# Second attention of a two-layer decoder: a running minimum, a scale moved into two other instructions, and GpSimd's work in another order

## The chip, the core and the metric
The kernel runs on one core of one Trainium2 chip. The metric is device time in microseconds, the median of three runs. TensorE multiplies matrices into PSUM, VectorE and ScalarE work on whole tiles (128 rows by so many columns) in PSUM or SBUF, GpSimd (POOL in the profile) on SBUF alone, SyncE (SP) issues DMA. Each engine works through its own queue in order and waits on semaphores for the others.

## The reference, cut to what matters
Two pre-norm decoder layers on 2048 tokens of width 256; each is attention and a feed-forward part. The change lies in the attention of the second layer, which has 16 heads over a latent of 64 columns, with a rotary part:

```
kv_c = x @ d_kv_w.T;  q_lat = x @ d_q_w.T          # 64 columns each
q = [u_q(q_lat), rope(qr(q_lat))];  k = [u_k(kv_c), rope(qr(kv_c))]
probs = softmax(q @ k.T / sqrt(128 + 64))           # 2048 x 2048, 16 heads, no mask
out = (probs @ u_v(kv_c)) @ out_w.T
```

## The kernel before, in words
The stage is `second_attention`. `prepare` makes the latents and folds the content part of query and key into one 64x64 matrix per head (`fold_hi`, `fold_lo`). Numbers that need more than one pass of precision are kept as a high part and a rest (`_hi`, `_lo`), so a product of two of them is three matmuls.

The main loop runs over 256 tiles: 16 heads by 16 blocks of 128 query rows. A tile's 2048 scores per row are worked on as two halves of 1024 columns, in a ring of three half-tiles in PSUM (`psS`). For tile n:

- TensorE: `scores(n+1, 0)`, `scores(n+1, 1)` (12 matmuls), one `project` piece of the next head in tiles 0 to 11 of a head, `context(n-2)` (32 pairs' worth of matmuls over the turned probabilities), and in the odd heads `output(n-9)`. Piece kinds 0 and 1 are rotated by VectorE; kind 2 is the fold, three matmuls over the 64 rows of the latent (lines 1585 to 1587).
- VectorE: `half(n+1, 0)` is the minimum of half 0 (the scores are negated) into `lows`; `low(n, 0)` subtracts the high part of half 0's probabilities; `half(n+1, 1)`; `whole_min(n+1)` takes the smaller of the two and adds 14 ln 2 as `shift`, so that the exponentials come out times 2^14; `rotate` for piece kinds 0 and 1; `invert(n-2)`; `low(n, 1)`.
- ScalarE: `exponential(n, 0)` (needs `shift`), `normalise(n-3)`, `take_output(n-10)`, `high(n, 0)` (the high part as f16), `exponential(n, 1)`, roundings and folds of the next head, `high(n, 1)`. `normalise(m)` waits until the splits of all tiles up to m-2 are done, since it writes one of two buffers of `both_sums`.
- GpSimd, the loop at the end of `gpsimd`: it waits for `low(n-1, 1)`, then adds a bias (first head) and an output (`add`), places weights in tile 14, waits for `low(n, 0)`, then one of `add_up` (two sums, `whole` of the queries and `whole_k` of the keys), `rest_queries` or `rest_keys`, by the remainder (i-2) mod 3 of the tile's number i in its head, for i from 2 to 13, and last `split(n-3)`: three small steps on `both_sums` and `ctxp`.
- SyncE: two transposes of the probabilities by DMA per tile, each waits for its `low`.

The subtractions of VectorE (`low`) read two tensors in SBUF; `half` and `rotate` read PSUM.

Of the kernel before, what the change touches and what calls it, by code (L numbers as in the profile page):

```python
# [44 lines left out]
def decoder_two_layers(nc, x_in, wq0, bq0, wk0, bk0, wv, bv, wout, bout, rwT, ewT, eb3, c_pick,  # L45
# [1080 lines left out]
    def second_attention():  # L1126
# [3 lines left out]
        LIFT = 14.0  # L1130
# [9 lines left out]
        fold_hi = sb(L, "fold_hi", [C, 1 + NH, C], F32R)  # L1140
        fold_lo = sb(L, "fold_lo", [C, 1 + NH, C], F32R)
# [28 lines left out]
        def prepare():  # L1170
# [84 lines left out]
            def vector():  # L1255
# [13 lines left out]
                for w in (fold_hi, fold_lo):  # L1269
                    ins = dve.tensor_scalar(w[:, 0, :], ident[0:C, 0:C], 0.0, None, ALU.mult)  # L1270
# [10 lines left out]
                def fold_rest(g):  # L1281
                    heads = slice(1 + 8 * g, 9 + 8 * g)
                    dve.wait_ge(fold_high, g + 1)
                    dve.scalar_tensor_tensor(out=fold_lo[:, heads, :], in0=six[4 + g][0:C, :].rearrange("p (h c) -> p h c", c=C),
                                             scalar=-SCALE, in1=fold_hi[:, heads, :].bitcast(F32), op0=ALU.mult,
                                             op1=ALU.subtract).then_inc(fold_low, 1)
# [61 lines left out]
            def scalar():  # L1348
# [29 lines left out]
                for g in range(2):  # L1378
                    act.wait_ge(fold_ready, g + 1)
                    act.activation(fold_hi[:, 1 + 8 * g:9 + 8 * g, :], six[4 + g][0:C, :].rearrange("p (h c) -> p h c", c=C),  # L1380
# [17 lines left out]
            def gpsimd():  # L1398
# [4 lines left out]
                pool.wait_ge(cleared, 1)  # L1403
                for j in range(NB):
# [47 lines left out]
        lows = sb(L, "lows", [P, 2, 2])  # L1452
# [112 lines left out]
        def tensor():  # L1565
            def project(head, piece):
# [166 lines left out]
        def vector():  # L1733
# [17 lines left out]
            def half(n, g):  # L1751
# [539 lines left out]
```

## Time and profile before
| | |
|---|---|
| time, median of 3 runs | 2437.64 us (2432.28 to 2438.07) |
| the profiled execution: time / span | 2436.7 / 2435.3 us |
| mean granted TensorE clock | 0.981 |
| second attention's main loop | from about 797 to 2240 us |
| busy, share of span | PE 90%, DVE 87%, ACT 75%, POOL 45% |

The rows below are copied from the trace of that execution. A line Lnnn is a line of the kernel before. Row durations of VectorE overlap a little: the next instruction can start before the row of the one before ends.

### The profile page before, as it was taken

To read this page: it belongs to the slowest core of one execution; us is meant where nothing else is said; L and a number is where in the kernel's file an instruction comes from. 1 tells how busy PE (TensorE), PEld (TensorE's weight loads), DVE (VectorE), ACT (ScalarE), POOL (GpSimd) and SP (SyncE) were. 2 spreads that over 40 slices of the span, in tenths; PEclk is the share of its full clock that TensorE was granted. 3 is DMA by queue.
4 is the path that set the end of the run, shared out by engine and by line. 5 is a ranking of instruction groups with operands and counts; after the bars stand their busy time and mean duration, and the time that the engine had idled before them with its cause. 6 is when DMAs were issued, how large, how long until landed. Compare 5 with 4: busy or idle time off the path is not lost.

```text
span 2435.3 us, 50686 instructions
## 1 busy us (share of the span) xinstructions
PE 2201.4 (90%) x18544; PEld 1583.4 (65%) x18544; DVE 2109.6 (87%) x3124; ACT 1822.2 (75%) x2613; POOL 1098.4 (45%) x1464
## 2 busy tenths in 40 slices
PE   4888888889997899999999999999999999988899
PEld 2444444455655667777777777767777777766687
DVE  6888888879987999999999999999999999987421
ACT  4777777745555788889888888888888888877411
POOL 3312111101224577657657667657666656622200
PEclk9999999989998999999999999999999999999899
DMA  3000000041000799999999999999999999999000
GB/s 130 1 2 2 1 1 2 2 87 32 1 1 1 137 193 196 195 193 198 195 195 194 194 195 193 187 194 195 194 198 191 196 196 199 205 195 191 21 18 18
DMA packets 1119318, 300.69 MB, mean 123 GB/s; under 512 B 1107232, under 2 KB 1116416, under 8 KB 1118208
## 3 DMA queue, kind: packets, MB, share of 16 engines
q1 hardware_dynamic: 1116224, 295.21, 69.8%
q8 instruction: 150, 2.46, 0.4%
q10 hardware_dynamic: 2848, 2.23, 0.3%
q14 instruction: 96, 0.79, 0.1%
HBM read 18.45 MB, written 2.10 MB: 8 GB/s over the span
## 4 chain that ended last, share of the span: by engine, by line
PE 28%; DVE 21%; issue 7%; DMA 6%; ACT 5%; POOL 1%; SPq 0%; DVEq 0%; ACTq 0%; POOLq 0%
DVE lows L1757 10%; DVE parts L1773 9%; DMA partsT<-parts 6%; PE psOb L1629 4%; PE psS L1612 4%; PE psS L1709 4%; PE psS L1614 3%; PE psS L1613 3%; ACT prob L1952 2%; PE psOb L1630 2%; PE psOb L1665 2%; ACT parts L1962 2%; PE psOb L1729 1%; PE psPb L1729 1%; PE psPb L1585 1%
## 5 line engine op out<-in xcount | busy, mean ns | idle before, releaser
L1773 DVE TENSOR_TENSOR parts<-prob,parts 128x1024 f16<-128x1024 f32 x512 | 679.9, 1328 | 18.9 <-ACT parts L1962 17.4
L1952 ACT ACTIVATE prob<-psS,shift 128x1024 f32<-128x1024 f32 x512 | 574.8, 1123 | 143.7 <-DVE shift L1765 139.0
L1757 DVE TENSOR_REDUCE lows<-psS 128x1 f32<-128x1024 f32 x512 | 622.4, 1216 | 5.6 <-PE psS L1614 5.0
L1962 ACT CAST parts<-prob 128x1024 f16<-128x1024 f32 x512 | 537.4, 1050 | 30.1 <-DMA partsT<-parts 26.2
L1612 PE MATMUL psS<-k_hi,q_lo 128*128 128x512 f32 x1024 | 446.7, 436 | 82.6 <-ACT prob L1952 75.2
L1629 PEld LDWEIGHTS psOb<-kv,partsT 128*128 128x128 f16 x4096 | 357.0, 97 | 99.0 <-issue 75.7
L1629 PE MATMUL psOb<-kv,partsT 128*128 128x130 f16 x4096 | 398.0, 221 | 20.1 <-DMA partsT<-parts 20.1
L1614 PE MATMUL psS<-k_hi,q_hi 128*128 128x512 f32 x1024 | 407.6, 398 | 0.0
L1613 PE MATMUL psS<-k_lo,q_hi 128*128 128x512 f32 x1024 | 405.5, 396 | 0.0
L1630 PE MATMUL psOb<-kv,partsT 128*128 128x66 f16 x4096 | 387.7, 193 | 0.0
L1630 PEld LDWEIGHTS psOb<-kv,partsT 128*128 128x128 f16 x4096 | 360.5, 98 | 1.0 <-issue 1.0
L665 ACT ACTIVATE PT<-psS 128x1024 bf16<-128x1024 f32 (+1 forms) x320 | 278.6, 899 | 64.8 <-PE psS L409 41.2
L1612 PEld LDWEIGHTS psS<-k_hi,q_lo 128*128 128x128 f32 x1024 | 194.0, 189 | 190.3 <-ACT prob L1952 154.9
L2086 POOL TENSOR_TENSOR both_sums<-both_sums 128x64 f32<-128x64 f32 x256 | 178.5, 697 | 164.3 <-DVE parts L1773 135.8
L1614 PEld LDWEIGHTS psS<-k_hi,q_hi 128*128 128x128 f32 x1024 | 193.7, 189 | 46.0
L1613 PEld LDWEIGHTS psS<-k_lo,q_hi 128*128 128x128 f32 x1024 | 195.2, 191 | 25.4
L737 POOL TENSOR_TENSOR qB<-nmT,blocks 32x512 bf16<-32x512 bf16 x64 | 73.5, 1148 | 301.3 <-DVE qB L540 298.7
L409 PE MATMUL psS<-qB,kT 128*128 128x512 bf16 (+3 forms) x640 | 180.0, 352 | 11.2 <-ACT PT L665 11.0
L524 DVE TENSOR_REDUCE pm<-psT 128x1 f32<-128x512 f32 (+3 forms) x256 | 156.7, 612 | 36.4 <-PE psT L383 23.9
L524 DVE TENSOR_REDUCE pm<-psU 128x1 f32<-128x512 f32 (+2 forms) x255 | 150.1, 589 | 22.8 <-PE psU L383 11.5
L2090 POOL TENSOR_TENSOR ctxp<-both_sums,ctxp 128x64 f16<-128x64 f32 x256 | 140.0, 547 | 20.5
L2056 POOL TENSOR_TENSOR whole<-rot 64x512 f32<-64x512 f32 x64 | 82.7, 1293 | 130.8 <-DVE parts L1773 124.4
(294 smaller groups left out, 3969.6 us busy)
## 6 DMA issues: line engine op xcount, KB each, us to landing
partsT<-parts SPq DMA_TRANSPOSE x512, 4.9
ef<-in_ewT SPq DMA_DIRECT2D x1, 2048.0 KB, 9.7
rf<-in_rwT SPq DMA_DIRECT2D x1, 2048.0 KB, 10.2
outw_s<-in_outwT SPq DMA_DIRECT2D x1, 2048.0 KB, 8.5
trig<-in_trig SPq DMA_DIRECT2D x2, 1024.0 KB, 11.5
out_x<-ot SPq DMA_DIRECT2D x16, 128.0 KB, 1.7
wug<-in_wupT SPq DMA_DIRECT2D x4, 256.0 KB, 3.7
wug<-in_wgateT SPq DMA_DIRECT2D x4, 256.0 KB, 3.9
```

The lines of the kernel that those rows point to most:

```text
L409: ins = pe.matmul(bank, kT[:, pair % 2, m * P:(m + 1) * P], qB[:, h, c * BANK + r * P:(c + 1) * BANK], start=True, stop=not diag)
L524: dve.tensor_reduce(pm[:, h, r, j:j + 1], max_banks[max_place[n["max"]]][:, 0:w], AX_X, ALU.max).then_inc(max_taken, 1)
L665: act.activation(PT[:, h, first:first + width], psS[:, x * BANK:x * BANK + width], ACT.Exp).then_inc(exp_done, 1)
L1612: pe.matmul(bank, q_lo[:, slot, q], k_hi[b][:, k], start=True, stop=False)
L1613: pe.matmul(bank, q_hi[:, slot, q], k_lo[b][:, k], start=False, stop=False)
L1614: ins = pe.matmul(bank, q_hi[:, slot, q], k_hi[b][:, k], start=False, stop=True)
L1629: pe.matmul(psO[:, 0:KW], partsT[:, s, 0, m, :], kv16[:, block, :], start=(block == 0), stop=False)
L1630: ins = pe.matmul(psO[:, 0:REST], partsT[:, s, 1, m, :], kv16[:, block, 0:REST], start=False, stop=(block == NT - 1))
L1757: dve.tensor_reduce(lows[:, n % 2, g:g + 1], psS[:, (2 * n + g) % 3, :], AX_X, ALU.min).then_inc(half_min, 1)
L1773: dve.tensor_tensor(parts[:, s, 1, :], prob[:, g, :], parts[:, s, 0, :], ALU.subtract).then_inc(low_done, 1)
L1952: act.activation(prob[:, g, :], psS[:, (2 * n + g) % 3, :], ACT.Exp, bias=shift[:, n % 2:n % 2 + 1], scale=-1.0).then_inc(exp_done, 1)
L1962: act.copy(parts[:, s, 0, :], prob[:, g, :]).then_inc(high_done, 1)
```

## The change
Four things. (1) `LIFT` is now the factor 2^14, applied as the scale of the cast (`high`, now an activation with Copy) and as the multiplier of the subtraction (`low`, now a multiply-subtract); the exponential itself is not lifted any more. (2) The small instruction `whole_min` is gone: half 0's minimum goes to `lows`, and half 1 is one pass that adds 0 to the scores, writes them back where they stand in PSUM and takes the running minimum from `lows` into its accumulator output, `shift`. (3) The folds run over 128 rows; the lower 64 rows of `fold_hi` and `fold_lo` are cleared by two copies on GpSimd in `prepare`. (4) GpSimd's order: the split of tile n-4 comes behind the second subtraction of tile n-1; the keys' sum is made one tile after the queries', as `add_up_keys`; the additions of outputs stand in one of two places.

```diff
-        LIFT = 14.0
+        LIFT = 2.0 ** 14
-        fold_hi = sb(L, "fold_hi", [C, 1 + NH, C], F32R)
+        fold_hi = sb(L, "fold_hi", [P, 1 + NH, C], F32R)
...
+                for w in (fold_hi, fold_lo):
+                    pool.tensor_copy(w[latent, :, :].rearrange("p a n -> p (a n)"), kvs[rotary, 0:(1 + NH) * C]).then_inc(pool_step.sem, 1)
+                    pool.wait_ge(pool_step.sem, pool_step.next())
...
-                    pe.matmul(bank, fl2, lat_hi[0:C, cols], start=True, stop=False)
-                    pe.matmul(bank, fh2, lat_lo[0:C, cols], start=False, stop=False)
-                    pe.matmul(bank, fh2, lat_hi[0:C, cols], start=False, stop=True).then_inc(piece_ready, 1)
+                    pe.matmul(bank, fl2, lat_hi[:, cols], start=True, stop=False)
+                    pe.matmul(bank, fh2, lat_lo[:, cols], start=False, stop=False)
+                    pe.matmul(bank, fh2, lat_hi[:, cols], start=False, stop=True).then_inc(piece_ready, 1)
...
-                if g == 0 and n >= 2:
-                    dve.wait_ge(shift_ready, n - 1)
-                dve.tensor_reduce(lows[:, n % 2, g:g + 1], psS[:, (2 * n + g) % 3, :], AX_X, ALU.min).then_inc(half_min, 1)
-
-            def whole_min(n):
-                if n >= TILES:
-                    return
-                dve.wait_ge(half_min, 2 * n + 2)
-                if n >= 2:
-                    dve.wait_ge(exp_done, 2 * n - 2)
-                dve.tensor_scalar(shift[:, n % 2:n % 2 + 1], lows[:, n % 2, 0:1], lows[:, n % 2, 1:2],
-                                  LIFT * float(np.log(2.0)), ALU.min, ALU.add).then_inc(shift_ready, 1)
+                here = psS[:, (2 * n + g) % 3, :]
+                if g == 0:
+                    if n >= 2:
+                        dve.wait_ge(shift_ready, n - 1)
+                    dve.tensor_reduce(lows[:, n % 2:n % 2 + 1], here, AX_X, ALU.min).then_inc(half_min, 1)
+                else:
+                    dve.wait_ge(half_min, n + 1)
+                    if n >= 2:
+                        dve.wait_ge(exp_done, 2 * n - 2)
+                    dve.tensor_scalar(here, here, 0.0, lows[:, n % 2:n % 2 + 1], ALU.add, ALU.min,
+                                      accum_out=shift[:, n % 2:n % 2 + 1]).then_inc(shift_ready, 1)
...
-                dve.tensor_tensor(parts[:, s, 1, :], prob[:, g, :], parts[:, s, 0, :], ALU.subtract).then_inc(low_done, 1)
+                dve.scalar_tensor_tensor(out=parts[:, s, 1, :], in0=prob[:, g, :], scalar=LIFT, in1=parts[:, s, 0, :],
+                                         op0=ALU.mult, op1=ALU.subtract).then_inc(low_done, 1)
...
-                act.copy(parts[:, s, 0, :], prob[:, g, :]).then_inc(high_done, 1)
+                act.activation(parts[:, s, 0, :], prob[:, g, :], ACT.Copy, scale=LIFT).then_inc(high_done, 1)
...
+            def add_up_keys(head, j):
                 if (head, j) == (1, 0):
                     pool.wait_ge(keys_rested, NB)
-                for side, (out_rows, rows) in enumerate(((whole, rotary), (whole_k, latent))[:2 if head else 1]):
-                    pool.tensor_tensor(out_rows[rotary, :], rot[0][rows, :], rot[1][rows, :], ALU.add).then_inc(added_up, 1)
-                    pool.wait_ge(added_up, sums(head, j) + side + 1)
+                pool.tensor_tensor(whole_k[rotary, :], rot[0][latent, :], rot[1][latent, :], ALU.add).then_inc(added_up, 1)
+                pool.wait_ge(added_up, sums(head, j) + 2)
...
-            for n in range(TILES + 3):
+            for n in range(TILES):
                 head, i = n // NT + 1, n % NT
                 j, turn = divmod(i - 2, 3)
-                ahead = n < TILES and head < NH
-                if n < TILES:
-                    pool.wait_ge(low_done, 2 * n)
+                ahead = head < NH and 2 <= i <= 13
+                pool.wait_ge(low_done, 2 * n)
+                if ahead and turn == 1:
+                    add_up_keys(head, j)
+                else:
+                    split(n - 4)
                 if n < NT:
                     add_bias(n)
-                add(n - LATER - 1)
-                if ahead and i == 14 and head + 1 < NH:
+                if not (ahead and turn):
+                    add(n - LATER - 1)
+                if i == 14 and head + 1 < NH:
                     take_weights(head + 1)
-                if n < TILES:
-                    pool.wait_ge(low_done, 2 * n + 1)
-                if ahead and 2 <= i <= 13 and turn == 0:
+                pool.wait_ge(low_done, 2 * n + 1)
+                if ahead and turn == 0:
                     add_up(head, j)
-                if ahead and 2 <= i <= 13 and turn == 1:
+                if ahead and turn == 1:
                     rest_queries(head, j, 2 * (n + 1))
-                if ahead and 2 <= i <= 13 and turn == 2:
+                    split(n - 4)
+                if ahead and turn == 2:
                     rest_keys(head, j)
+                if ahead and turn:
+                    add(n - LATER - 1)
+            split(TILES - 4)
+            for n in range(TILES, TILES + 3):
+                add(n - LATER - 1)
                 split(n - 3)
```

## Rows read from the trace of the kernel before

**Rows 1.** Page, part 1: engine, busy us (share of span), instructions
```profile
PE 2201.4 (90%) x18544; PEld 1583.4 (65%) x18544; DVE 2109.6 (87%) x3124; ACT 1822.2 (75%) x2613; POOL 1098.4 (45%) x1464
```

**Rows 2.** Page, part 5: groups; busy us, mean ns of one, idle before, releaser
```profile
L1773 DVE TENSOR_TENSOR parts<-prob,parts 128x1024 f16<-128x1024 f32 x512 | 679.9, 1328 | 18.9 <-ACT parts L1962 17.4
...
L1757 DVE TENSOR_REDUCE lows<-psS 128x1 f32<-128x1024 f32 x512 | 622.4, 1216 | 5.6 <-PE psS L1614 5.0
L1962 ACT CAST parts<-prob 128x1024 f16<-128x1024 f32 x512 | 537.4, 1050 | 30.1 <-DMA partsT<-parts 26.2
```

**Rows 3.** Timeline of VectorE, tile 131: start us, duration us, engine, line, operation
```profile
1538.77 1.71 DVE L1773 TENSOR_TENSOR parts<-prob,parts 128x1024 f16<-128x1024 f32 x1
1540.40 1.21 DVE L1757 TENSOR_REDUCE lows<-psS 128x1 f32<-128x1024 f32 x1
1541.65 0.21 DVE L1765 TENSOR_SCALAR shift<-lows 128x1 f32<-128x1 f32 x1
1541.78 0.74 DVE L1742 SCALAR_TENSOR_TENSOR rot<-psPb,br,trig 128x512 f32<-128x512 f32 x1
...
1542.52 1.21 DVE L1773 TENSOR_TENSOR parts<-prob,parts 128x1024 f16<-128x1024 f32 x1
1543.64 1.22 DVE L1757 TENSOR_REDUCE lows<-psS 128x1 f32<-128x1024 f32 x1
...
1547.16 0.21 DVE L1765 TENSOR_SCALAR shift<-lows 128x1 f32<-128x1 f32 x1
```

**Rows 4.** Timeline of GpSimd, the same tile and just before
```profile
1535.35 1.29 POOL L2056 TENSOR_TENSOR whole_k<-rot 64x512 f32<-64x512 f32 x1
...
1538.66 0.74 POOL L2101 TENSOR_TENSOR x<-x,part 128x256 f32<-128x256 f32 x1
1540.61 1.28 POOL L2065 TENSOR_TENSOR q_lo<-whole,q_hi 128x512 fp32r<-128x512 f32 x1 [1.21 <-DVE parts L1773]
...
1542.67 1.22 POOL L2090 TENSOR_TENSOR ctxp<-both_sums,ctxp 128x64 f16<-128x64 f32 x1
```

**Rows 5.** Timeline of ScalarE, the same tile
```profile
1541.90 1.11 ACT L1952 ACTIVATE prob<-psS,shift 128x1024 f32<-128x1024 f32 x1 [1.17 <-DVE shift L1765]
1542.91 0.36 ACT L1971 ACTIVATE both_sums<-psOb,rden 128x128 f32<-128x128 f32 x1
1543.16 0.48 ACT L1986 ACTIVATE part<-psOb,kv_unit 128x256 f32<-128x256 f32 x1
1543.52 1.05 ACT L1962 CAST parts<-prob 128x1024 f16<-128x1024 f32 x1
```

**Rows 6.** Shifts: two in the last head, and all (min/median/max ns, first and last)
```profile
2180.46 0.21 DVE L1765 TENSOR_SCALAR shift<-lows 128x1 f32<-128x1 f32 x1
...
2185.44 0.21 DVE L1765 TENSOR_SCALAR shift<-lows 128x1 f32<-128x1 f32 x1
...
L1765 DVE TENSOR_SCALAR shift<-lows x256: 212/214/217, 801.6 to 2238.0; 128x1 f32<-128x1 f32 x128
```

**Rows 7.** Groups by form, VectorE, 0 to 1150 us: two-input operations
```profile
L967 DVE TENSOR_TENSOR under<-psE,second 128x1024 bf16<-128x1024 f32 x32 | 39.0, 1217 | 0.0
...
L1303 DVE SCALAR_TENSOR_TENSOR qr_lo<-qr_s,scale_col,qr_hi 128x1024 fp32r<-128x1024 f32 x2 | 2.6, 1284 | 0.1
L1284 DVE SCALAR_TENSOR_TENSOR fold_lo<-psS,fold_hi 64x512 fp32r<-64x512 f32 x2 | 1.3, 677 | 2.0 <-ACT fold_hi L1380 2.0
```

**Rows 8.** Groups by form, ScalarE, 0 to 820 us: accumulator read, scaled copy
```profile
L1041 ACT ACTIVATION_READ_ACCUMULATOR weight<-psE 128x1 f32 x128 | 28.3, 221 | 0.0
...
L1380 ACT ACTIVATE fold_hi<-psS 64x512 fp32r<-64x512 f32 x2 | 1.1, 574 | 0.0
```

**Rows 9.** Groups by form, TensorE, 1150 to 2050 us: projection and fold
```profile
L1580 PE MATMUL psPb<-lat_hi,wr_lo 128*128 128x512 f32 x80 | 31.6, 396 | 0.0
...
L1585 PE MATMUL psPb<-lat_hi,fold_lo 64*128 64x512 f32 x40 | 19.9, 497 | 0.0
```

More of the change, by code:

```diff
@@ L1139, in second_attention @@
             k_lo.append(sb(L, f"k_lo{b}", [P, T], F32R))
[L1140 to L1141 removed]
+        fold_hi = sb(L, "fold_hi", [P, 1 + NH, C], F32R)
+        fold_lo = sb(L, "fold_lo", [P, 1 + NH, C], F32R)
         KW, ONE, REST = 2 * C + 2, C, C + 2
@@ L1269, in vector @@
                 for w in (fold_hi, fold_lo):
-                    ins = dve.tensor_scalar(w[:, 0, :], ident[0:C, 0:C], 0.0, None, ALU.mult)
+                    ins = dve.tensor_scalar(w[0:C, 0, :], ident[0:C, 0:C], 0.0, None, ALU.mult)
                 ins.then_inc(filled, 1)
@@ L1283, in fold_rest @@
                     dve.wait_ge(fold_high, g + 1)
-                    dve.scalar_tensor_tensor(out=fold_lo[:, heads, :], in0=six[4 + g][0:C, :].rearrange("p (h c) -> p h c", c=C),
-                                             scalar=-SCALE, in1=fold_hi[:, heads, :].bitcast(F32), op0=ALU.mult,
+                    dve.scalar_tensor_tensor(out=fold_lo[0:C, heads, :], in0=six[4 + g][0:C, :].rearrange("p (h c) -> p h c", c=C),
+                                             scalar=-SCALE, in1=fold_hi[0:C, heads, :].bitcast(F32), op0=ALU.mult,
                                              op1=ALU.subtract).then_inc(fold_low, 1)
@@ L1379, in scalar @@
                     act.wait_ge(fold_ready, g + 1)
-                    act.activation(fold_hi[:, 1 + 8 * g:9 + 8 * g, :], six[4 + g][0:C, :].rearrange("p (h c) -> p h c", c=C),
+                    act.activation(fold_hi[0:C, 1 + 8 * g:9 + 8 * g, :], six[4 + g][0:C, :].rearrange("p (h c) -> p h c", c=C),
                                    ACT.Copy, scale=-SCALE).then_inc(fold_high, 1)
@@ L1451, in second_attention @@
         part = sb(L, "part", [P, D])
-        lows = sb(L, "lows", [P, 2, 2])
+        lows = sb(L, "lows", [P, 2])
         shift = sb(L, "shift", [P, 2])
@@ L2052, in add_up @@
                     pool.wait_ge(rests_done, sums(head, j))
+                pool.tensor_tensor(whole[rotary, :], rot[0][rotary, :], rot[1][rotary, :], ALU.add).then_inc(added_up, 1)
+                pool.wait_ge(added_up, sums(head, j) + 1)
+            def add_up_keys(head, j):
                 if (head, j) == (1, 0):
                     pool.wait_ge(keys_rested, NB)
-                for side, (out_rows, rows) in enumerate(((whole, rotary), (whole_k, latent))[:2 if head else 1]):
-                    pool.tensor_tensor(out_rows[rotary, :], rot[0][rows, :], rot[1][rows, :], ALU.add).then_inc(added_up, 1)
-                    pool.wait_ge(added_up, sums(head, j) + side + 1)
+                pool.tensor_tensor(whole_k[rotary, :], rot[0][latent, :], rot[1][latent, :], ALU.add).then_inc(added_up, 1)
+                pool.wait_ge(added_up, sums(head, j) + 2)
             def rest_queries(head, j, halves_scored):
@@ L2118, in gpsimd @@
             take_weights(1)
-            for n in range(TILES + 3):
+            for n in range(TILES):
                 head, i = n // NT + 1, n % NT
                 j, turn = divmod(i - 2, 3)
-                ahead = n < TILES and head < NH
-                if n < TILES:
-                    pool.wait_ge(low_done, 2 * n)
+                ahead = head < NH and 2 <= i <= 13
[4 more added lines that the diff above has]
+                    split(n - 4)
                 if n < NT:
                     add_bias(n)
-                add(n - LATER - 1)
-                if ahead and i == 14 and head + 1 < NH:
-                    take_weights(head + 1)
-                if n < TILES:
-                    pool.wait_ge(low_done, 2 * n + 1)
-                if ahead and 2 <= i <= 13 and turn == 0:
-                    add_up(head, j)
-                if ahead and 2 <= i <= 13 and turn == 1:
-                    rest_queries(head, j, 2 * (n + 1))
-                if ahead and 2 <= i <= 13 and turn == 2:
-                    rest_keys(head, j)
+                if not (ahead and turn):
+                    add(n - LATER - 1)
+                if i == 14 and head + 1 < NH:
+                    take_weights(head + 1)
+                pool.wait_ge(low_done, 2 * n + 1)
+                if ahead and turn == 0:
+                    add_up(head, j)
+                if ahead and turn == 1:
+                    rest_queries(head, j, 2 * (n + 1))
+                    split(n - 4)
+                if ahead and turn == 2:
+                    rest_keys(head, j)
+                if ahead and turn:
+                    add(n - LATER - 1)
+            split(TILES - 4)
+            for n in range(TILES, TILES + 3):
+                add(n - LATER - 1)
                 split(n - 3)
```

2 lines of the change are left out of this document (removed).

## The prediction
> **What bounds the kernel now.** I read the page's busy shares first: VectorE 87% of the span and TensorE 90% [rows 1]. The costliest groups then say where: the subtraction, the minimum and the cast of the second attention, 512 instructions each, lead it [rows 2]. From the code, tile n has two halves, and per tile VectorE runs, in this order: minimum of half 0 of tile n+1, subtraction of half 0, minimum of half 1, the small shift, a rotation in half of the tiles, a reciprocal, subtraction of half 1. The timeline of VectorE through one tile shows it packed: minimum at 1540.40, shift at 1541.65, rotation at 1541.78, subtraction at 1542.52, next minimum at 1543.64, each starting 0.08 to 0.1 us before its forerunner's row ends or 0.03 us behind it [rows 3].
>
> The last six clean tiles give the pace without rotation: shift at 2180.46, the next at 2185.44, so 4.98 us; with a rotation it is 5.51 (1541.65 to 1547.16), which I carry as 5.50 [rows 3, 6]. Where a tile also takes an output, ScalarE has 0.36 us more in its chain (copy `part` starts 1543.16, the cast 1543.52 [rows 5]), which makes about 5.37 us of a tile without rotation. The 256 shifts run from 801.6 to 2238.0, 1436.4 us for 255 steps [rows 6]. Eight tiles of each of the 15 heads that prepare a next one have a rotation (120); of the other 135, 56 take an output (heads in pairs, seven pairs, eight each). By those paces: 120 x 5.50 + 56 x 5.37 + 79 x 4.98 = 1354 us. So 82 us are lost to something. I put about 22 of them on what stays (the last tiles beside the weight loads, one single gap, the start), and 60 on collisions of GpSimd with the subtractions and TensorE coming late behind them.
>
> The collision can be read. A subtraction alone takes about 1.21 us; the one at 1538.77 took 1.71, and GpSimd's addition had begun at 1538.66 and ended at 1539.40 [rows 3, 4]. The other way round, GpSimd's last split step started at 1542.67, just behind the subtraction of 1542.52, and took 1.22 instead of the 0.31 it takes free: it ended 0.16 behind the subtraction [rows 3, 4]. So the two exclude each other, and whoever starts first makes the other wait; minima and rotations, which read PSUM, run beside GpSimd undisturbed.
>
> **The change part by part.** All sums are against the profiled execution (span 2435.3, time 2436.7), 0.9 us under the median of the runs, 2437.64.
>
> *Scaling in the cast and the subtraction.* The cast becomes a copy with an immediate scale. Such a copy of 64x512 takes 574 ns [rows 8], and the present cast is 1050 ns for twice the columns [rows 2]; I take nothing, bounds 0 and +0.03 us. The subtraction gets an immediate multiplier. With an immediate, 64x512 took 677 ns; with a per-partition scalar and two SBUF inputs, 128x1024 took 1284 against 1217 for a plain two-input operation [rows 7]. I take no change; the upper bound is 0.07 us, or 36 us over 512. The Trainium skill speaks against this edit: Vector Engine (DVE) Microarchitecture Reference, Points that are easy to get wrong, says that this instruction form with two non-bf16 SBUF sources runs at half throughput. That would be another 1.1 us in each of 512 subtractions. The 1284 ns row is such an instruction at full rate [rows 7], so I give this rule only 2 in 100.
>
> *Running minimum.* Removed: per tile one reduction of 1.216 us, and the shift, which starts 1.25 behind the reduction's start (it waits for it) and runs 0.21. From reduction start to exponential start 1.50 us (1540.40 to 1541.90), to the next vector instruction 1.38 [rows 3, 5]. Added: one pass over 128x1024 with a per-partition scalar that writes PSUM back, and a read of the accumulator. No row shows either on VectorE. The pass is bounded by 1.21 (plain reduction or two-input operation) and 1.28 (with a per-partition scalar) [rows 2, 7], the write into PSUM is unseen and could cost more. ScalarE's read of its accumulator is 0.22 us [rows 8]; the short vector rows of a column are 0.21 [rows 3]. With 1.28, 0.09 overlap and a 0.15 read, the exponential starts 1.19 + 0.15 + 0.04 = 1.38 behind the start and the next vector instruction at about 1.30. So 0.08 to 0.12 is saved per tile; I take 0.08. The bounds are a saving of 0.20 (1.21 and a 0.06 read) and a loss of 0.20 (a PSUM write of 0.2 to 0.3 more). Over some 240 tiles that are bound by VectorE or by the chain through it: 19 us saved, between 48 saved and 48 lost.
>
> *Folds over 128 rows.* The first fold matmul takes 497 ns against 396 for a full-height one [rows 9], and there are 60 in the loop. The whole is at most 0.3 us a time on TensorE, and in these tiles TensorE waits for exponentials anyway; 0, bound 18 us saved. The clearing of the lower rows is two GpSimd copies in preparation, where it waits for latents: nothing.
>
> *GpSimd's order, what it removes.* Splits and the key sum no longer pile up behind the first subtraction of a tile: the 60 us above go. Only what the new order brings comes back, below.
>
> *What it brings, ScalarE's wait.* The normalisation of tile m waits until the splits up to m-2 are done. Before, split n-3 ran in turn n, one turn ahead of need. Now split n-4 runs in turn n. In most turns it opens the turn and is early enough. In the turn after the piece sum (turn remainder 1; tiles 3, 6, 9, 12 of 15 heads, so 60 tiles) it stands behind `q_lo`, and the next tile's normalisation needs exactly this split. The trace shows this sequence with its times, as the order there is the same: take L, the end of the first subtraction, 1538.77 + 1.71 = 1540.48. `q_lo` starts at L+0.13, the third split step is locked out by the subtraction and ends at 1543.89 = L+3.41 [rows 3, 4]. The next tile's normalisation starts at 1542.91 = L+2.43 [rows 5]. It would have to wait until L+3.45: 1.0 us. ScalarE's queue is in order: behind it stand the copy of an output, the cast of half 0 and with it the next tile's first subtraction, the exponential of half 1 and its scores' bank.
> From L: cast start L+3.71, end 4.75, subtraction 4.79. VectorE would be ready at 2.04 (the second subtraction, 1542.52), plus 1.12 to the next minimum, plus 1.13 behind that: 4.30 [rows 3]. Idle 0.49 us in 24 tiles with rotation and no output; 0.88 with the output's copy, 21 tiles; and in the 15 tiles 12, without rotation, where ScalarE's chain is the pace already, the full 1.05. 24 x 0.49 + 21 x 0.88 + 15 x 1.05 = 46 us. Lower bound 0 (see the rivals), upper bound 60 x 1.05 = 63.
>
> *Key sum behind the second subtraction.* It starts 0.13 to 0.22 behind it and takes 1.30 [rows 4], so it ends at about 1.46; the subtraction of half 0 wants to read at 1.05 + 0.12 = 1.17 [rows 3]. 0.29 x 60, less what tile 12's slack hides: 16 us.
> *Additions before the second half.* In the 21 turns with an output and remainder 2 the key rest and the addition end about 0.34 into the subtraction, 7 us; others 3. The bias additions of head 0, which now stand between, 4. Weight placing stays as it is, 6. Together 20.
>
> Sum: -60 + 46 + 16 + 20 = +22; running minimum -19; +3 in all. 2436.7 + 3 = 2440 us. The DMA transposes keep step: at 4.98 us a tile they did.
>
> **Rivals.**
> 1. ScalarE's wait is not there or is absorbed. Needed is only that the third split step gets in before the subtraction; it started at 1542.67 against 1542.52 [rows 3, 4], so 0.15 us decide, in all 60. For it: in tiles where TensorE's output comes late the subtraction is late too. Against it: the faster minimum moves the subtraction earlier still. Without the 46: 2394; with half of it 2417. I centre it on 2400.
> 2. The running minimum costs more than it saves: writing 128x1024 back to PSUM and reading the accumulator take longer than 1.46 us together instead of 1.34. It is on VectorE and in front of ScalarE's exponential. Without any saving the sum is 2459; from a saving below 0.06 us a tile on it decides the sign (2445). At a loss of 0.05 a tile it gives 2471, at 0.12 2488. For it: no row shows such a write. Against: every vector row of 1024 columns with a PSUM source lies at 1.21 to 1.22 [rows 2, 7].
> The Trainium skill (VectorE: DVE Perf Modes, Two Vector instructions with no wait between them) says an operation with accumulator output is two instructions. This trace shows it for ScalarE alone [rows 8]; it is what I priced.
> 3. The running minimum is much cheaper (saving 0.2): 2440 - 29 = 2411.
> 4. The multiply-subtract at half rate, by the mechanism weighed above: 512 x 1.1 = 563 us more, 3003.
>
> **How the numbers follow.** Forecast 0.46 (own range 2426 to 2456); rival 1, 0.23; rival 2, 0.17; rival 3, 0.12; rival 4, 0.02. About 0.3% (7.3 us) is what a measurement of this kernel tells from no change. Below 2430: rivals 1 and 3 (0.35) and a little of the forecast, 0.39. Above 2445: rivals 2 and 4 (0.19) and a good third of the forecast, 0.35. Between, 0.26. The range of 8 in 10 takes rival 1's centre and most of rival 2: 2396 to 2476.
>
> **What would show it.** (a) ScalarE's normalisation waiting for GpSimd's `ctxp`, about 1 us, 60 times; if that row is missing, rival 1. (b) The new pass at about 1.28 and an accumulator row; exponential start 1.38 behind its start. (c) The multiply-subtract's mean near 1.25, from 1.33. (d) First subtractions of 1.5 us beside the key sum. (e) No 1.7 to 2.1 us subtractions in remainder 0 turns. (f) Fold's first matmul at 0.40. I am wrong if shift to shift without rotation is over 5.0 us, or if the wait of (a) is there and VectorE still loses nothing.

## The result, and the profile after
The changed kernel takes 2456.05 us (median; 2453.16 to 2458.17) against 2436.7 beside it: ratio 1.0081, 95% interval 1.0068 to 1.0094. That is slower by 19 us, which the interval tells from no change, and 16 us above the forecast of 2440. The profiled execution has a span of 2453.8 us and a granted clock of 0.984 (before 2435.3 and 0.981).

The page's busy shares of the changed kernel, which answer to [rows 1]:

```profile
PE 2190.8 (89%) x18544; PEld 1584.3 (65%) x18544; DVE 2073.0 (84%) x3124; ACT 1834.6 (75%) x2613; POOL 1012.4 (41%) x1466
```

VectorE has 37 us less to do than before and the kernel still takes 19 more. The page's groups say where the time sits, beside [rows 2]:

```profile
L1775 DVE SCALAR_TENSOR_TENSOR parts<-prob,parts 128x1024 f16<-128x1024 f32 x512 | 674.3, 1317 | 97.7 <-ACT parts L1963 94.4
...
L1963 ACT ACTIVATE parts<-prob 128x1024 f16<-128x1024 f32 x512 | 542.2, 1059 | 21.6 <-DMA partsT<-parts 17.8
...
L1767 DVE TENSOR_SCALAR_CACHE_REDUCE psS<-psS,lows 128x1024 f32<-128x1024 f32 x256 | 328.4, 1283 | 1.8 <-PE psS L1617 1.8
...
L1762 DVE TENSOR_REDUCE lows<-psS 128x1 f32<-128x1024 f32 x256 | 310.8, 1214 | 3.6 <-PE psS L1617 3.0
...
L1972 ACT ACTIVATE both_sums<-psOb,rden 128x128 f32<-128x128 f32 x256 | 92.6, 362 | 75.2 <-POOL ctxp L2094 73.4
```

VectorE stands idle 97.7 us before its subtractions, 94.4 of them for ScalarE's cast; before it was 18.9 and 17.4. The last row shown tells why the cast is late: the normalisation (L1972) waits 73 us for the last step of GpSimd's split (L2094). The view of the waits, main loop (800 to 2240 us; engine, what waited, for whom: us, times, longest), gives the number of times and shows a second wait of ScalarE on GpSimd, which the prediction didn't name:

```profile
DVE parts L1775 <- ACT parts L1963: 92.8, 85, 2.7
...
ACT both_sums L1972 <- POOL ctxp L2094: 73.4, 59, 1.6
...
ACT part L1987 <- POOL x L2105: 15.0, 28, 0.8
```

Tile 131, the same as in [rows 3 to 5], in the timelines of VectorE, GpSimd and ScalarE (start us, duration us; in brackets what the engine had waited, and for whom):

```profile
1564.88 1.76 DVE L1775 SCALAR_TENSOR_TENSOR parts<-prob,parts 128x1024 f16<-128x1024 f32 x1
1566.57 1.28 DVE L1767 TENSOR_SCALAR_CACHE_REDUCE psS<-psS,lows 128x1024 f32<-128x1024 f32 x1
1567.77 0.13 DVE L1767 DVE_READ_ACCUMULATOR psS<-psS,lows 128x1 f32 x1
...
1568.51 1.20 DVE L1775 SCALAR_TENSOR_TENSOR parts<-prob,parts 128x1024 f16<-128x1024 f32 x1
1569.63 1.21 DVE L1762 TENSOR_REDUCE lows<-psS 128x1 f32<-128x1024 f32 x1
...
1572.55 1.22 DVE L1775 SCALAR_TENSOR_TENSOR parts<-prob,parts 128x1024 f16<-128x1024 f32 x1 [1.71 <-ACT parts L1963]
```
```profile
1564.28 1.28 POOL L2060 TENSOR_TENSOR whole_k<-rot 64x512 f32<-64x512 f32 x1 [1.53 <-DVE parts L1775]
1566.78 1.28 POOL L2069 TENSOR_TENSOR q_lo<-whole,q_hi 128x512 fp32r<-128x512 f32 x1 [1.22 <-DVE parts L1775]
...
1568.52 1.28 POOL L2092 CAST ctxp<-both_sums 128x64 f16<-128x64 f32 x1
1569.89 0.31 POOL L2094 TENSOR_TENSOR ctxp<-both_sums,ctxp 128x64 f16<-128x64 f32 x1
1570.27 0.73 POOL L2105 TENSOR_TENSOR x<-x,part 128x256 f32<-128x256 f32 x1
```
```profile
1567.94 1.12 ACT L1953 ACTIVATE prob<-psS,shift 128x1024 f32<-128x1024 f32 x1 [0.69 <-DVE psS L1767]
...
1570.29 0.37 ACT L1972 ACTIVATE both_sums<-psOb,rden 128x128 f32<-128x128 f32 x1 [1.23 <-POOL ctxp L2094]
1571.10 0.48 ACT L1987 ACTIVATE part<-psOb,kv_unit 128x256 f32<-128x256 f32 x1 [0.44 <-POOL x L2105]
1571.47 1.05 ACT L1963 ACTIVATE parts<-prob 128x1024 f16<-128x1024 f32 x1
```

With L = 1566.64, the end of the first subtraction: `q_lo` (L+0.14) stands ahead of the split. The middle split step runs into the subtraction of 1568.51 and takes 1.28 us; the third ends at L+3.56. The exponential had ended at L+2.42; ScalarE starts its normalisation at L+3.65, 1.23 us late. The output's copy behind it waits 0.44 us more, since the addition that frees `part` comes behind that split too. The cast ends at L+5.88 and VectorE has stood idle 1.71 us. The wait for the split comes back behind the turns of remainder 1 (60 turns; the row above has it 59 times), the second one where the tile takes an output.

**Where the 20 us are.** I added up the rows of VectorE's timeline from the first `shift` to the last (255 tiles): the loop's length, the gaps over 0.03 us between rows ("idle"), what is left ("work"), and by how much the subtractions exceed 1.225 us, which is about their median in every kernel ("lost in subtractions"). The changed kernel against the one before: 20 = 60 more idle, 40 less work, 6 of these from the subtractions. The 60 have two sources. The changed kernel with GpSimd's old order has 26 more idle time than the kernel before, the new order adds 33. And the order's part sits where the tile above has it: in the 59 tiles behind a turn of remainder 1 VectorE is idle 74 us before its first subtraction (7 in the old order, 5 before), 1.63 us in each of the 28 that take an output and 0.92 in the other 31. The same sums for the kernels of the next section:

| kernel | median, us | loop | idle | work | lost in subtractions |
|---|---|---|---|---|---|
| before | 2436.7 | 1436.4 | 52.5 | 1383.9 | 53.6 |
| before, new order only | 2478.6 | 1476.8 | 109.6 | 1367.2 | 33.7 |
| before, 128-row folds only | 2429.4 | 1431.5 | 46.2 | 1385.3 | 53.5 |
| before, running minimum only | 2426.0 | 1425.9 | 72.4 | 1353.5 | 51.8 |
| changed | 2456.1 | 1456.5 | 112.3 | 1344.2 | 47.5 |
| changed, old order | 2423.6 | 1425.6 | 78.9 | 1346.7 | 47.1 |
| changed, first wait removed | 2435.8 | 1437.2 | 93.3 | 1343.9 | 47.9 |
| changed, second wait removed | 2437.6 | 1438.2 | 98.8 | 1339.4 | 40.9 |
| changed, split ahead of `rest_queries` | 2439.2 | 1436.3 | 74.5 | 1361.8 | 66.5 |
| changed, both waits removed | 2422.9 | 1422.5 | 75.8 | 1346.7 | 46.6 |
| the same, half the transposes' bytes | 2370.6 | 1370.1 | 22.7 | 1347.5 | 53.2 |
| old order, half the bytes | 2377.1 | 1377.6 | 32.7 | 1344.9 | 49.6 |
| changed, half the bytes | 2440.8 | 1441.6 | 97.0 | 1344.6 | 48.8 |
| both waits removed, each transpose in two | 2530.8 | 1534.2 | 185.8 | 1348.4 | 28.9 |

### The profile page after: what moved, and what is told of

The parts are those of the page before. It is cut to its first block, busy times and chain, and to the rows that moved or that the text cites. A ratio compares the mean times of both kernels' runs of the same rounds, so it can differ in the third digit from the quotient of the medians.

```text
span 2453.8 us, 50819 instructions
## 1 busy us (share of the span) xinstructions
PE 2190.8 (89%) x18544; PEld 1584.3 (65%) x18544; DVE 2073.0 (84%) x3124; ACT 1834.6 (75%) x2613; POOL 1012.4 (41%) x1466
## 3 DMA queue, kind: packets, MB, share of 16 engines
q8 instruction: 150, 2.46, 0.4%
## 4 chain that ended last, share of the span: by engine, by line
PE 21%; DVE 16%; issue 9%; ACT 8%; POOL 7%; DMA 6%; SPq 0%; DVEq 0%; POOLq 0%; ACTq 0%
DVE parts L1775 6%; DMA partsT<-parts 6%; DVE psS L1767 5%; PE psOb L1632 4%; PE psS L1712 4%; DVE lows L1762 3%; ACT prob L1953 3%; ACT parts L1963 3%; POOL q_lo L2069 3%; PE psS L1615 2%; PE psOb L1668 2%; PE psOb L1633 2%; POOL ctxp L2092 2%; PE psS L1617 2%; PE psS L1616 2%
## 5 line engine op out<-in xcount | busy, mean ns | idle before, releaser
L1775 DVE SCALAR_TENSOR_TENSOR parts<-prob,parts 128x1024 f16<-128x1024 f32 x512 | 674.3, 1317 | 97.7 <-ACT parts L1963 94.4
L1963 ACT ACTIVATE parts<-prob 128x1024 f16<-128x1024 f32 x512 | 542.2, 1059 | 21.6 <-DMA partsT<-parts 17.8
L1767 DVE TENSOR_SCALAR_CACHE_REDUCE psS<-psS,lows 128x1024 f32<-128x1024 f32 x256 | 328.4, 1283 | 1.8 <-PE psS L1617 1.8
L1762 DVE TENSOR_REDUCE lows<-psS 128x1 f32<-128x1024 f32 x256 | 310.8, 1214 | 3.6 <-PE psS L1617 3.0
L2090 POOL TENSOR_TENSOR both_sums<-both_sums 128x64 f32<-128x64 f32 x256 | 97.2, 380 | 307.6 <-DVE parts L1775 276.0
L737 POOL TENSOR_TENSOR qB<-nmT,blocks 32x512 bf16<-32x512 bf16 x64 | 73.4, 1147 | 301.2 <-DVE qB L540 298.6
L1972 ACT ACTIVATE both_sums<-psOb,rden 128x128 f32<-128x128 f32 x256 | 92.6, 362 | 75.2 <-POOL ctxp L2094 73.4
```

Of the source, the lines that this page charges most:

```text
L1762: dve.tensor_reduce(lows[:, n % 2:n % 2 + 1], here, AX_X, ALU.min).then_inc(half_min, 1)
L1767: dve.tensor_scalar(here, here, 0.0, lows[:, n % 2:n % 2 + 1], ALU.add, ALU.min, accum_out=shift[:, n % 2:n % 2 + 1]).then_inc(shift_ready, 1)
L1775: dve.scalar_tensor_tensor(out=parts[:, s, 1, :], in0=prob[:, g, :], scalar=LIFT, in1=parts[:, s, 0, :], op0=ALU.mult, op1=ALU.subtract).t ...
L1963: act.activation(parts[:, s, 0, :], prob[:, g, :], ACT.Copy, scale=LIFT).then_inc(high_done, 1)
```

## The experiments
Each kernel's ratio is to the kernel before, run beside it on the same chip (2434.2, 2434.7, 2435.0 and 2435.9 us). Differences between two changed kernels are those of their medians; as the kernel before itself moved between 2434.2 and 2436.7 us, they are good to 2 or 3 us.

**The first wait alone.** A third buffer for the normalised sums, on the changed kernel:

```diff
-        both_sums = sb(L, "both_sums", [P, 2, 2, C])
+        both_sums = sb(L, "both_sums", [P, 3, 2, C])
...
-                if n >= 2:
-                    act.wait_ge(ctx_split, 3 * (n - 1))
+                if n >= 3:
+                    act.wait_ge(ctx_split, 3 * (n - 2))
...
-                mean = both_sums[:, n % 2, 0, :]
+                mean = both_sums[:, n % 3, 0, :]
...
```

> The changed kernel with three buffers of both_sums in place of two, so that the normalisation of tile m waits for the splits up to m-3; GpSimd's order and everything else stay. Theory W (the new order makes ScalarE wait for the splits, and this is what costs): in the changed kernel ScalarE waits 75 us before the normalisation and VectorE 94 us before its subtractions (17 before). Here both_sums<-ctxp waits vanish, the subtraction's idle falls below 35 us, and the time is about 2395 (2380 to 2412). Rival C (GpSimd's new order collides more with the subtractions, or the pass with accumulator costs): the wait only moves elsewhere, VectorE stays late, 2440 or more.

2435.8 us, 1.0006 (0.9996 to 1.0015): 20 us back of the 61 that were expected. The waits of this kernel:

```profile
DVE parts L1775 <- ACT parts L1963: 69.9, 66, 3.3
ACT part L1987 <- POOL x L2105: 43.0, 28, 2.0
ACT parts L1963 <- DMA partsT<-parts: 35.1, 31, 3.3
```

The row of the normalisation is gone; its neighbour has grown from 15.0 to 43.0 us, with the same count of 28. ScalarE now waits one instruction later for the addition, as this stretch of its timeline shows:

```profile
1559.29 0.36 ACT L1972 ACTIVATE both_sums<-psOb,rden 128x128 f32<-128x128 f32 x1
...
1561.43 0.48 ACT L1987 ACTIVATE part<-psOb,kv_unit 128x256 f32<-128x256 f32 x1 [1.79 <-POOL x L2105]
```

**The order alone.** GpSimd's order of before on the changed kernel, and the new order on the kernel before; `add_up` and the loop at the end of `gpsimd` change places as whole blocks:

```diff
-                if ahead and turn == 1:
-                    add_up_keys(head, j)
-                else:
-                    split(n - 4)
...
+                if n < TILES:
+                    pool.wait_ge(low_done, 2 * n + 1)
...
+                split(n - 3)
```

> The changed kernel with GpSimd's loop and sums as they were before; running minimum, scaled cast and multiply-subtract, folds over 128 rows stay. Theory W: the three arithmetic edits save about 0.11 us a tile, 2437 - 28 = 2409 (2400 to 2420), and the order alone costs 47. Rival C in its second form (the pass with accumulator costs more than the pair it replaces): 2437 or more.

2423.6 us, 0.9955 (0.9940 to 0.9969), 4 us above the range that was expected. On the changed arithmetic the new order costs 32 us, and the arithmetic alone gives 11, not 28.

> The kernel before with GpSimd's new order alone. Theory W: all of the loss is here, 2437 + 40 = 2477 (2465 to 2490), with ScalarE waiting for ctxp about 60 us. Rival C (the loss is in the arithmetic edits): within 0.3% of the kernel before, 2430 to 2444.

2478.6 us, 1.0178 (1.0163 to 1.0194). On the old arithmetic it costs 44, though here it does take 20 us out of the subtractions (53.6 to 33.7).

**The split ahead of `rest_queries`** in turn remainder 1:

```diff
-                    rest_queries(head, j, 2 * (n + 1))
                     split(n - 4)
+                    rest_queries(head, j, 2 * (n + 1))
```

> The changed kernel with two lines exchanged: in the 60 tiles of turn remainder 1 the split comes before rest_queries. Theory W: ScalarE's wait for the split goes (75 us to under 10), but q_lo now ends 0.5 us into the second subtraction in 45 tiles and is locked out by it in 15, which gives back about 22: 2456 - 50 = 2406 (2390 to 2425). Rival C: q_lo's collision comes on top of what is there, 2460 to 2480.

2439.2 us, 1.0015 (1.0004 to 1.0025): 17 us back of the 50 that were expected. The wait for the split goes (0.9 us left; VectorE idle 74.5 us, from 112.3), but the one for the addition grows, from 15.0 us, as it did with three buffers (800 to 2240 us):

```profile
ACT part L1987 <- POOL x L2105: 41.0, 28, 1.9
```

And `q_lo`, of 1.28 us, now runs where the small steps ran: it is under way at the start of 44 slow second subtractions, which lose 24 us (before the exchange 8, which lost 2.5), and all subtractions lose 66.5 us instead of 47.5. The loop gains 20.

**Both waits.** `both_sums` in three buffers, and the output's copy in two:

```diff
-                if outputs(n):
-                    act.wait_ge(out_added, outputs(n))
-                act.activation(part[:, :], psO[:, BANK // 2:BANK], ACT.Copy, scale=kv_unit[:, 0:1]).then_inc(out_taken, 1)
+                if outputs(n) > 1:
+                    act.wait_ge(out_added, outputs(n) - 1)
+                act.activation((part, bias_row)[outputs(n) % 2][:, :], psO[:, BANK // 2:BANK], ACT.Copy, scale=kv_unit[:, 0:1]).then_inc(out_taken, 1)
...
```

> The changed kernel with three buffers of both_sums and, beside that, two buffers for the output's copy (part and the row of the bias, which is free after head 0). With three buffers alone, in the tiles behind turn remainder 1 that take an output a tile still takes 7.13 us, and ScalarE waits 43 us in 28 tiles for GpSimd's addition x<-x,part. Theory W2 (the order makes ScalarE wait twice, for the split and for the addition, and the second hides behind the first): these 28 tiles fall to 5.6 to 5.8 us, 28 x 1.4 = 39 us less than with three buffers alone: 2436 - 39 = 2397 (2388 to 2410). Rival (the time in these tiles is TensorE's or the lock's, and the wait would be hidden): 2428 or more.

2422.9 us, 0.9948 (0.9933 to 0.9963): 33 us are back, and the kernel equals the old order's (2423.6; the intervals overlap). Expected was 2397. Its waits:

```profile
ACT parts L1963 <- DMA partsT<-parts: 64.9, 57, 3.0
...
PE psOb L1632 <- DMA partsT<-parts: 45.9, 43, 3.5
DVE parts L1775 <- ACT parts L1963: 31.6, 51, 2.8
```

No wait on GpSimd is left in ScalarE's queue. The casts now wait for the DMA transposes that read their buffer's last contents: 64.9 us, from 13.9 in the changed kernel and 26.2 before. The old order on the changed arithmetic has the same row:

```profile
ACT parts L1963 <- DMA partsT<-parts: 58.7, 63, 3.0
```

**The second wait alone**, by the second of those edits without the first:

> The changed kernel with two buffers for the output's copy alone (two of both_sums). Theory W2: the wait for the addition lies behind the wait for the split in ScalarE's queue, 15 us of it visible; taking it away alone gives 5 to 15: 2441 to 2451. If the addition's wait is independent of the split's, about 25 to 40: 2416 to 2431.

2437.6 us, 1.0012 (1.0002 to 1.0021), between the two ranges that were expected. Each edit alone gives 18 to 20 us, both 33. That this is less than their sum is not shown: the sum is 39 by the medians and 35 by the ratios, and the intervals cover the difference.

```profile
DVE parts L1775 <- ACT parts L1963: 75.5, 80, 2.7
ACT both_sums L1972 <- POOL ctxp L2094: 74.6, 59, 1.6
...
ACT parts L1963 <- DMA partsT<-parts: 20.4, 20, 3.3
```

The normalisation's wait stays at 74.6 us, as long as with one copy (73.4). The 28 tiles with an output fall from 45.7 to 34.3 us of VectorE's idle time; the table has 7 of the gain in the subtractions, which the edit doesn't touch.

**Are the transposes the floor?** From tile 4 on only the high part of each half is transposed. All other instructions stay and read the rests of earlier tiles, so this kernel leaves out a part of the result and serves as a probe alone:

```diff
+                if n < 4:
                     sp.dma_start_transpose(partsT[:, s, :, :, :].rearrange("p a m q -> p (a m) q"),
                                            parts[:, s, :, :].rearrange("p a k -> p (a k)")).then_inc(landed[s], 16)
+                else:
+                    sp.dma_start_transpose(partsT[:, s, 0, :, :], parts[:, s, 0, :]).then_inc(landed[s], 16)
```

On the changed kernel with the old order:

> The changed kernel with GpSimd's old order (2423.6 us), where from tile 4 on the DMA turns only the high part of the probabilities, half of the bytes; the rests of later tiles stay those of the first ones, so the output is not the reference's. That kernel came out 15 us above what its shorter vector work promised, and ScalarE there waits 59 us for transposes (30 before). Theory D (the DMA is the next bound): these waits vanish and the time falls by 10 to 15, to 2408 to 2414. Rival G (the missing 15 us are new collisions with GpSimd, as VectorE's work lies 0.1 us earlier to it): 2419 to 2425.

2377.1 us, 0.9760 (0.9746 to 0.9775): 46 us less by the DMA alone, where 10 to 15 were expected. The transposes' rows of both kernels (SP's queue: min/median/max ns of a row; then issue to landing), half the bytes first:

```profile
L2153 SPq DMA_TRANSPOSE partsT<-parts x502: 1231/1232/2552, 831.2 to 2187.1; - x168
...
DMA to landing us min/median/max: 3.0/3.1/5.2
```
```profile
L2149 SPq DMA_TRANSPOSE partsT<-parts x491: 1317/2456/4399, 827.9 to 2198.4; - x164
...
DMA to landing us min/median/max: 4.3/4.9/7.0
```

A whole transpose lands 4.9 us behind its issue, and two are issued in a tile of about 5. With half the bytes no cast waits for a transpose any more. On the kernel with both waits removed, and on the changed kernel itself:

> Three buffers of both_sums, two for the output's copy, and half of the transposes' bytes left out as before (rests of later tiles stay old, output not the reference's). Both waits gone gave 2422.9 instead of 2397, and ScalarE then waited 65 us for transposes. Theory D (the gain of freed waits is turned into waits for the DMA): 2422.9 falls by 45 to 60, to 2363 to 2378, level with or below the old order under the same cut (2377). Rival L (the new order itself still costs in GpSimd's collisions, and the DMA only hides that): clearly above 2377, 2385 or more.

> The changed kernel with the same cut of the transposes and nothing else. Theory W and D: ScalarE's waits for split and addition keep this kernel so slow that the DMA keeps step (18 us of waits), so the cut gives only 10 to 20: 2436 to 2446, and against the kernel with both waits gone the order's waits then cost about 70 instead of 33. Rival (the DMA is the bound of the changed kernel too): 2410 to 2420, as much as in the other orders.

2370.6 us (0.9738, 0.9723 to 0.9753) and 2440.8 us (1.0027, 1.0017 to 1.0036). With half the bytes the two waits are worth 70 us; with all of them 33. So the order's loss and the transposes' don't add up: in the kernel that VectorE and ScalarE hold up, the transposes are hardly waited for (13.9 us). The changed kernel itself gains only 15 from them, as its waits stay what they were:

```profile
DVE parts L1775 <- ACT parts L1963: 89.0, 83, 2.1
...
ACT both_sums L1972 <- POOL ctxp L2094: 73.2, 59, 1.6
ACT part L1987 <- POOL x L2105: 15.1, 28, 0.8
```

**The other two parts alone.** The kernel before with the running minimum, the scaled cast and the multiply-subtract:

> The kernel before with the running minimum, the scaled cast and the multiply-subtract alone (old order of GpSimd, folds over 64 rows). With the order old and all three arithmetic edits it was 2423.6. If the folds give nothing by themselves, this is 2421 to 2426. If the folds are what gives the gain, it is 2432 or more.

2426.0 us, 0.9960 (0.9945 to 0.9975), 9 less. VectorE's work falls by 30 us in the table, and its idle time rises by 20. The casts' wait for the transposes tells of it (26.2 before):

```profile
ACT parts L1960 <- DMA partsT<-parts: 46.6, 55, 3.5
```

The kernel before with the folds over 128 rows:

> The kernel before with the folds over 128 rows alone. The prediction gave this 0 to 18 us, taking 0: 2432 to 2436. If TensorE's 0.2 to 0.33 us in 60 tiles lie on the path in the half of the tiles with an output, 2426 to 2431.

2429.4 us, 0.9982 (0.9973 to 0.9992), 4 to 5 less. Its first fold matmul, TensorE by form, 1150 to 2050 us, against 497 ns in [rows 9]:

```profile
L1588 PE MATMUL psPb<-lat_hi,fold_lo 128*128 128x512 f32 x40 | 15.7, 392 | 0.0
```

**An attempt at a better kernel.** On the kernel with both waits removed each half is transposed in two, the high part as soon as its cast is done:

```diff
-                sp.wait_ge(low_done, 2 * n + g + 1)
+                sp.wait_ge(high_done, 2 * n + g + 1)
...
-                sp.dma_start_transpose(partsT[:, s, :, :, :].rearrange("p a m q -> p (a m) q"),
-                                       parts[:, s, :, :].rearrange("p a k -> p (a k)")).then_inc(landed[s], 16)
+                sp.dma_start_transpose(partsT[:, s, 0, :, :], parts[:, s, 0, :]).then_inc(landed[s], 16)
+                sp.wait_ge(low_done, 2 * n + g + 1)
+                sp.dma_start_transpose(partsT[:, s, 1, :, :], parts[:, s, 1, :]).then_inc(landed[s], 16)
...
```

> Three buffers of both_sums, two for the output's copy, and each half's transpose issued as two: the high part behind the cast, the rest behind the subtraction, the same bytes in all. With half the bytes a transpose landed in 3.1 us in place of 4.9 and held its queue 1.23 in place of 2.4, so two of them hold the queue as long, but the second starts into an emptier one. Theory D, latency form (what waits is the landing behind the subtraction): ScalarE's waits for transposes fall from 65 to under 30 us and the time from 2422.9 to 2385 to 2410. Rival Q (the queue is full by its issue time, four times 1.23 = 4.9 us of a 5.3 us tile, and the split helps nothing or hurts): 2420 to 2445.

2530.8 us, 1.0381 (1.0358 to 1.0405): 108 us more than without the edit, and 86 above the worse of the two ranges that were expected. The page's group of the cast and its row of the DMA issues:

```profile
L1963 ACT ACTIVATE parts<-prob 128x1024 f16<-128x1024 f32 x512 | 542.2, 1059 | 220.0 <-DMA partsT<-parts 214.9
...
partsT<-parts SPq DMA_TRANSPOSE x1024, 3.4
```

Each piece lands sooner (3.4 us) and there are twice as many; the casts wait 215 us for them. SP's queue is then hardly ever free: from 850 to 2190 us 831 of 889 transposes start less than 0.1 us behind the row before, and the rows fill 92% of the time, at 1.38 us each in the mean, so that four take 5.5 us, where a tile took 5.6 without the edit. With half the bytes (two small ones a tile) the rows fill 45 to 49%. That this edit makes the kernel slower is shown. Which part of it does, the number of transposes or the earlier issue of the high part, is not, nor whether the rows are long by SP's queue or by the DMA engines behind it: the two large ones of a tile fill 92% too in the kernel without the edit.

## Why the forecast came near, and which step failed
The sum was -60 + 46 + 16 + 20 for the order, -19 for the running minimum, together +3. The median rose by 19. By the table the parts are: subtractions -6, where -60 + 16 + 20 = -24 was forecast; idle time +60, where +46 was; the rest of VectorE's work -34, where -19 was. The errors of 18 and 14 us add and the one of 15 goes against them, so that the time is 16 or 17 us off. That they left no more than this is in part luck, since by cause they are larger: the order's collisions are 24 us and the arithmetic's idle time 26 us to the bad, the order's idle time 13 and the arithmetic's work 18 to the good. Two slips of addition in the prediction weigh under 2 us each: 4.98 + 0.36 is 5.34, not 5.37, and 0.49 + 0.36 is 0.85, not 0.88.

**The failed step: "Splits and the key sum no longer pile up behind the first subtraction of a tile: the 60 us above go."** Two things were wrong with it. The size was a remainder (82 minus 22), though it could be read: (1328 - 1224) ns in 512 subtractions are 53 us, with the mean of [rows 2] and this median from the kernel before:

```profile
L1773 DVE TENSOR_TENSOR parts<-prob,parts x512: 1202/1224/2330, 804.1 to 2245.0; 128x1024 f16<-128x1024 f32 x171
```
And they didn't go. I took the 92 slow subtractions of before (1.4 us or more), and looked which GpSimd row ran as each began: 32 stood against `whole_k` (27 us lost), 42 against an addition (18), 18 against `q_lo` or `k_lo` (8). In the changed kernel there are 142: 53 against `whole_k`, now at the first subtraction and 0.2 us each (11 us), 28 against `whole` (14), 39 against an addition (15), 22 against `q_lo` or `k_lo` (7). A GpSimd row that has been kept out by one subtraction pushes what follows it into the next. The turn before tile 131 shows it. The addition stood ahead of `add_up` before too, but now the split stands in front of it; so it begins just behind the start of a subtraction (1559.75 and 1559.58) and takes 1.63 us, so that `whole` starts late and still runs when the second subtraction begins, which takes 1.58:

```profile
1559.58 1.21 DVE L1775 SCALAR_TENSOR_TENSOR parts<-prob,parts 128x1024 f16<-128x1024 f32 x1
1559.75 1.63 POOL L2105 TENSOR_TENSOR x<-x,part 128x256 f32<-128x256 f32 x1
...
1561.46 1.28 POOL L2054 TENSOR_TENSOR whole<-rot 64x512 f32<-64x512 f32 x1
...
1562.24 1.58 DVE L1775 SCALAR_TENSOR_TENSOR parts<-prob,parts 128x1024 f16<-128x1024 f32 x1
```

These 28 are in the turns of remainder 0, which the prediction held free of slow subtractions; 20 of them take 1.7 to 1.83 us, against its sign (e). Sign (d), 1.5 us beside the key sum, came as 1.4 us and more, 53 times. With the changed arithmetic the order takes nothing from the subtractions (47.1 in the old order, 47.5 in the new, 46.6 without the waits); only with the old arithmetic it took 20. The Trainium skill (SBUF — State Buffer, Who interferes with whom) states the rule for it: a VectorE instruction with two SBUF inputs contends with GpSimd instructions that read SBUF, and the first to start keeps the other out. The rows agree: the split's cast at 1568.52 in tile 131, just behind the subtraction, took 1.28 us, and the addition above 1.63, where [rows 4] have 0.74 for one that began first.

**ScalarE's wait for the split: the mechanism was right, its size was not.** Forecast: 60 times, 1.0 us, split end at L+3.41, idle 0.49 to 1.05 us in a tile and 46 in all. Seen: 59 in the window, 1.24 us in the mean (73.4 / 59), end at L+3.56, idle 0.92 us in a tile without an output, 1.63 with one (forecast 0.88), and 74 in these tiles. What was missing is the next instruction's wait: the output's copy waits for an addition that the new order puts behind the split. Its own row is small (15.0 us), but removing the first wait turned it into 43.0, and only with both gone came the 33 us. Rival 1 is out, since the third step never got in ahead of the subtraction, in none of the 60 turns. Of the 67 us that these tiles gain over the old order the whole loop keeps only 33 as idle time, since VectorE then waits less elsewhere (before its reciprocal, for TensorE's context: 13 us, from 34). So the order's +22 and the 32 us that it costs come apart like this: the collisions are 24 us worse than the sum had them (nothing in place of -24), its idle time 13 us better (33 in place of 46).

**"The DMA transposes keep step: at 4.98 us a tile they did."** This failed too, and hid itself. The kernel before already had 26.2 us of such waits [rows 2]; in the changed kernel ScalarE waits only 13.9 us for them. As soon as a cut makes the tile shorter the row comes up: 46.6 us with the running minimum alone, 58.7 in the old order, 64.9 without the waits, and half the bytes give 46 to 52 us. At 2423 us they are part of what sets the pace.

**The running minimum.** The pass is 1.28 us, as taken, the read of the accumulator 0.14 (taken 0.15); both stand in the tile above. Start of pass to start of exponential is 1.37 us (forecast 1.38; before 1.50). From one shift to the next it is, in undisturbed tiles, 4.88 us without a rotation (before 4.98) and 5.37 with one (before 5.50), so 0.10 to 0.13 saved against 0.08, and 30 to 35 us of VectorE's work against 19. With the running minimum and the scaling alone only 9 reach the time, since the idle time rises by 20, for which the sum had no term. Rivals 2 and 3 are out: the pass costs neither more nor much less. The Trainium skill (VectorE: DVE Perf Modes, Two Vector instructions with no wait between them) has the accumulator's output as an instruction of its own; the trace agrees, with 256 rows of 138 ns.

**The multiply-subtract and the scaled cast** cost nothing: median 1226 against 1224 ns, cast 1059 against 1050 (5 us in 512, beside other work).

```profile
L1775 DVE SCALAR_TENSOR_TENSOR parts<-prob,parts x512: 1195/1226/1833, 803.2 to 2264.3; 128x1024 f16<-128x1024 f32 x171
```

Rival 4 is out by the same row. The half throughput that the Trainium skill (Vector Engine (DVE) Microarchitecture Reference, Points that are easy to get wrong) gives for this form isn't seen with one f32 and one f16 source in SBUF; the measurement decides.

**The folds** were put at 0 and gave 4 to 5 us (interval 2 to 7), within the bound of 18. The order was forecast at +22 and is at +32; the arithmetic with the folds at -19 and is at -11, as 37 us less work were followed by 26 us more idle time.

What stays open: by which resource the transposes are slow (SP's queue or the DMA engines); why the order takes 20 us out of the subtractions on the old arithmetic and none on the new; and of the 26 us of idle time that came with the arithmetic, how much is the transposes' (the casts' wait for them grew by 33 us in the old order, from 26.2 to 58.7).

## What to carry to other kernels
Before a work item is moved in the queue of an engine that seems to be idle, list every semaphore that it feeds, and look at the tightest buffer behind each: here a ring of two and a single buffer made a move cost 32 us, and one more buffer for each gave it back. Read the size of a loss from rows (mean less median, times the count) and not as a remainder, and ask with whom the moved item collides next. And test what lies beneath the bound: a wait that showed 14 us here hid one of 65, worth some 50 us of the time, once the others were gone.

## What the runs showed of the hardware that was not expected
- A wait can keep another small: the casts' wait for the transposes was 26.2 us before, 13.9 in the changed kernel and 64.9 with the two waits removed; the two waits were worth 33 us beside full transposes and 70 beside half ones.
- A DMA transpose of 128x2048 f16 elements held SP's row 2.46 us in the median (1.32 the shortest) and landed after 4.9, one of 128x1024 held it 1.23 (1.23 the shortest) and landed after 3.1. Two of the small ones in place of a large one, the first issued earlier, made the kernel 4.5% slower (2422.9 to 2530.8 us).
- A pass over 128x1024 in PSUM that writes its result back to PSUM and accumulates took 1.283 us, against 1.214 for the reduction that only reads.
- What a collision costs a subtraction, over its 1.225 us, is how much of GpSimd's row is left when it begins, less 0.14 us: so in each of the 92 slow subtractions before and the 142 in the changed kernel, to within 0.01 us. `whole_k`, 1.29 us long, had 0.98 us left before and cost VectorE 0.84 in the mean (27 us in 32); in the changed kernel it had 0.35 left and cost 0.21 (11 us in 53).
